# Block 0's normalisation placed inside the end of the mixture, in a two-layer macaron kernel

## The chip, the cores and the metric

One core of one Trainium2 chip runs the whole program. The metric is the device time of one launch in microseconds (us); lower is better. The core has five engines that run their own instruction streams and meet only at semaphores: TensorE (PE in the profile, with its weight loads as PEld), VectorE (DVE), ScalarE (ACT), GpSimd (POOL) and SyncE (SP), which only issues transfers here.

## The reference

The input is 2 sequences of 2048 tokens with 256 features. Every residual branch starts from a layer norm:

```python
x = x + 0.5 * moe(norm(x))      # layer 0, "ffn0a": 32 experts, 4 per token, 160 slots each, and a shared expert
x = x + gla(norm(x))            # layer 0, "attn0": gated linear attention
x = x + 0.5 * moe(norm(x))      # "ffn0b", the weights of ffn0a
x = x + 0.5 * ffn1(norm(x))     # layer 1, "ffn1a": 8 experts, 2 per token
x = x + attn1(norm(x))          # layer 1, a scan over time
x = x + 0.5 * ffn1(norm(x))     # "ffn1b"
```

Of `moe`, this matters: each expert's output rows are scaled and added to their tokens, and the shared expert's output `silu(x @ gate.T) * (x @ up.T) @ down.T` is added for every token.

## The kernel before

Tokens lie on 128 partitions, 32 tiles deep, in `main_x`; 4 tiles are a block, so there are 8 blocks (`NB`). Each stage is a `Block` in which every engine has a list of instructions written by hand; a barrier of all engines stands between two stages. Two such seams matter here: ffn0a to attn0 (whose first half is `project`) and ffn0b to ffn1a. ffn0a and ffn0b are the same code, `moe`.

In `moe` blocks 0, 1, 4, 5, 6, 7 go through the shared expert first (`up`, `gate`, `hidden`, `down`, `keep`; `NF` = 6), then come 32 routed experts, then the shared expert for the two late blocks 2 and 3. Routed outputs can't be added to `main_x`, whose space holds expert weights (`we`) and shared outputs by then, so they are added in HBM, to four tables `ffn_sums`: GpSimd issues 40 scattered adds (`add`, L693), one per piece of 128 rows. Expert e goes to table e % 4; the four tables are complete one after another.

The late part in TensorE's order is: up products of a late block (`up`, L763, into the banks of `ps_a` and `ps_b`), its down products (`down`, L773, into `ps_c` and `ps_d`), and the same again. ScalarE takes the silu (L949), VectorE multiplies (`hidden`, L1069), ScalarE copies the output to `main_x` (`keep_late`, L955). While this runs, SyncE waits for the last pieces of each table and loads block 0 of it (`sp_first`, L1264, two transfers per table) into `main_spare`.

After the barrier, VectorE adds the four tables of block 0 (`dve_first`, L1278, L1281, L1286), takes its statistics (L216, L221); GpSimd turns the variance into 1/deviation (L245 to L248). In attn0 VectorE then writes the normed block (L232), in ffn1a ScalarE does (L2109); TensorE transposes it (L265), ScalarE copies the transpose out of PSUM (L276, L2118), and the first real products follow (L1540 in attn0, L2191 in ffn1a). Blocks 1 to 7 come through `combine.sp` (L1271, eight transfers a block, each half released by VectorE's adds of the block before) and `combine.dve` (L1295, L1304, for late blocks L1300 and L1302). Before block 0's transposes TensorE runs ten passes of products that nobody reads (`warm`, L177), and in attn0 joins two small gate weights (`join_gate_weights`, L1583 and L1587).

Early in ffn0a, SyncE's list is: clear tables (L410), store shared outputs (`shared`, L599), and load the first two groups of expert weights (`load`, L602, 1.5 MB each). `shared_y` has two places: ScalarE's copy for output n waits for the store of output n - 2. SyncE's list has `load(0)` and `load(1)` ahead of `shared(3)`. In ffn0b the loads stand earlier in the list.

## Time and profile before

| | us |
|---|---|
| three timed runs, lowest / median / highest | 1153.76 / 1155.86 / 1157.72 |
| the profiled execution's own time | 1156.85 |
| span of its instructions | 1154.9 |
| TensorE busy | 1023.1 |
| VectorE busy | 723.8 |
| ScalarE busy | 560.0 |
| GpSimd busy | 383.0 |

The profiled execution's own time is 1.95 above its span and 0.99 above the median of the timed runs. Times in the rows count from the start of the span. A row of a timeline is: start, duration, engine, line, operation, what it writes and reads, how many, and in brackets how long its engine had been idle and who released it. PEclk is the granted clock of TensorE as a share of its upper level, so 1.00 is 2.4 GHz and 0.50 is 1.2 GHz.

### The profile page before, as it was taken

The page shows a single profiled execution, that of the slowest core. Times are in us where ns is not written, and L with a number is a line of the kernel's source. Part 1 is how long each engine was busy: PE and PEld are TensorE (multiplying, and loading weights), DVE is VectorE, ACT ScalarE, POOL GpSimd, SP SyncE. Part 2 cuts the span into 40 slices and gives each one's busy share as a digit, 9 for nine tenths or more (in the row PEclk, how much of TensorE's full clock was granted, in tenths as well). Part 3 has the DMA queues.
Part 4 walks back from the last instruction along what each step waited for, and adds up shares of the span by engine and source line. Part 5 has one row for each costly group of instructions (what it writes and reads, how often), then busy time and mean ns, then how long its engine had stood idle before and what let it go on. Part 6 is the DMA issues. An engine that isn't in the chain of part 4 may idle for free. (4 is left out here: it accounts for less than half of the span.)

```text
span 1154.9 us, 17176 instructions
## 1 busy us (share of the span) xinstructions
PE 1023.1 (89%) x5110; PEld 606.1 (52%) x5128; DVE 723.8 (63%) x2529; ACT 560.0 (48%) x1071; POOL 383.0 (33%) x448
## 2 busy tenths in 40 slices
PE   7998899969998799989998989857887799985997
PEld 4755666535565466656666666423333456642343
DVE  4598432147884566754797331168876699964885
ACT  6621333325665745548422333246664655525884
POOL 3006777700000232314017887311101256521110
PEclk9999899999999799999999999968889899997998
DMA  9849987834440802005428887575400000000012
GB/s 326 331 159 306 185 199 182 183 113 146 151 141 13 324 37 91 11 28 173 165 73 157 201 234 132 104 230 181 141 5 1 1 0 1 1 1 0 20 54 73
DMA packets 81127, 140.72 MB, mean 122 GB/s; under 512 B 17776, under 2 KB 48864, under 8 KB 78944
## 3 DMA queue, kind: packets, MB, share of 16 engines
q1 hardware_dynamic: 65696, 117.58, 29.4%
q0 software_dynamic: 15360, 22.29, 13.0%
q8 instruction: 33, 0.54, 0.2%
q14 instruction: 38, 0.31, 0.1%
HBM read 82.17 MB, written 58.72 MB: 122 GB/s over the span
## 5 line engine op out<-in xcount | busy, mean ns | idle before, releaser
L693 POOL DMA_INDIRECT ffn_sums<-ffn0a_xT,ffn0a_into x40 | 62.7, 1567 | 16.0 <-issue 8.8
L693 POOL DMA_INDIRECT ffn_sums<-ffn0b_xT,ffn0b_into x40 | 62.5, 1563 | 14.7 <-issue 9.2
L1721 POOL TENSOR_TENSOR attn_attend_state_m<-attn_attend_state,attn_attend_heads 128x512 f32<-128x512 f32 x15 | 19.1, 1272 | 87.3 <-DVE attn_attend_state L1763 81.8
L2593 PE MATMUL attn_ps_k<-attn_xk,mixing_wk 128*128 128x512 f32 (+1 forms) x96 | 46.7, 610 | 0.0
L2598 PE MATMUL attn_ps_r<-attn_xr,mixing_wr 128*128 128x512 f32 (+1 forms) x96 | 45.2, 593 | 0.7 <-DVE attn_out L2462 0.7
L1143 DVE TENSOR_TENSOR ffn0a_h<-ffn0a_sg,ffn0a_ps_b 128x160 f32<-128x160 f32 x32 | 10.3, 322 | 54.4 <-ACT ffn0a_sg L981 54.3
L2608 PE MATMUL attn_ps_y<-mixing_wv,attn_out 128*128 128x256 f32 (+1 forms) x192 | 43.0, 380 | 1.2 <-DVE attn_out L2462 1.2
L842 PE MATMUL ffn0a_ps_b<-main_x,ffn0a_h 128*32 128x256 f32 (+2 forms) x144 | 43.5, 403 | 0.0
L842 PE MATMUL ffn0b_ps_b<-main_x,ffn0b_h 128*32 128x256 f32 (+2 forms) x144 | 43.5, 403 | 0.0
L820 PE MATMUL ffn0a_ps_b<-ffn0a_early,main_x 128*128 128x160 f32 x256 | 41.3, 305 | 2.1 <-DMA main_x<-w_experts 1.8
L1742 DVE COPY_PREDICATED main_spare<-attn_attend_causal,attn_attend_ps_a 128x1024 f32<-128x1024 int32 x32 | 40.3, 1312 | 4.6 <-issue 3.0
L1143 DVE TENSOR_TENSOR ffn0b_h<-ffn0b_sg,ffn0b_ps_b 128x160 f32<-128x160 f32 x32 | 10.3, 321 | 52.4 <-ACT ffn0b_sg L981 52.3
L2608 PEld LDWEIGHTS attn_ps_y<-mixing_wv,attn_out 128*128 128x128 f32 (+1 forms) x192 | 36.3, 190 | 10.1 <-issue 3.3
L820 PE MATMUL ffn0b_ps_b<-ffn0b_early,main_x 128*128 128x160 f32 x256 | 41.3, 305 | 0.3 <-ACT ffn0b_early L974 0.3
L820 PEld LDWEIGHTS ffn0a_ps_b<-ffn0a_early,main_x 128*128 128x128 f32 x256 | 36.6, 190 | 7.7 <-issue 3.5
L820 PEld LDWEIGHTS ffn0b_ps_b<-ffn0b_early,main_x 128*128 128x128 f32 x256 | 36.6, 190 | 5.7 <-issue 4.2
L2452 DVE TENSOR_TENSOR_SCAN attn_st<-mixing_keep,attn_carry,attn_kr 128x512 f32<-128x512 f32 (+1 forms) x24 | 32.1, 1337 | 9.8 <-ACT attn_kr L2553 9.7
L773 PE MATMUL ffn0a_ps_c<-ffn0a_shared_down,ffn0a_h 128*128 128x256 f32 x112 | 29.0, 405 | 9.8 <-ACT main_x L966 6.9
L1295 DVE TENSOR_TENSOR main_spare<-main_spare 128x1024 f32<-128x1024 f32 x28 | 34.1, 1218 | 4.9 <-DMA main_spare<-ffn_sums 4.9
L1763 DVE SCALAR_TENSOR_TENSOR attn_attend_state<-attn_attend_state,attn_decay,attn_attend_ps_s 128x256 f32<-128x256 f32 x32 | 14.0, 478 | 33.2 <-PE attn_attend_ps_s L1861 33.2
L395 POOL DMA_INDIRECT ffn0a_early<-ffn_rows,ffn0a_token x10 | 12.6, 1256 | 63.5 <-issue 63.2
L1876 PE MATMUL attn_attend_ps_w<-attn_attend_wo,attn_attend_cent 128*128 128x256 f32 x128 | 31.6, 391 | 2.1 <-DVE attn_attend_cent L1757 2.1
(510 smaller groups left out, 2718.9 us busy)
## 6 DMA issues: line engine op xcount, KB each, us to landing
main_spare<-ffn_sums SPq DMA_DIRECT2D x128, 256.0 KB, 3.6
main_x<-w_experts SPq DMA_DIRECT2D x16, 1536.0 KB, 7.1
ffn_sums<-main_lent SPq DMA_DIRECT2D x36, 512.0 KB, 6.3
ffn_sums<-main_x SPq DMA_DIRECT2D x28, 512.0 KB, 4.6
ffn_rows<-ffn0a_early SPq DMA_DIRECT2D x8, 512.0 KB, 9.7
ffn_rows<-ffn0b_early SPq DMA_DIRECT2D x8, 512.0 KB, 2.9
x_out<-main_x SPq DMA_DIRECT2D x8, 512.0 KB, 2.9
main_x<-x_in SPq DMA_DIRECT2D x3, 1024.0 KB, 10.7
```

Source lines behind the costliest of these rows:

```text
L693: g.indirect_dma_start(out=sums[:, :], out_offset=IndirectOffsetOnAxis(ap=into[:, at, j:j + 1], axis=0), in_=ys[:, n % NY, :], in_offset=N ...
L773: ins = mm(ps[:, i, :], h[:, n % 2, m, t * P:(t + 1) * P], wd[:, m, :], start=m == 0, stop=m == 1)
L820: ins = mm(ps_b[:, p, j * CAP:(j + 1) * CAP], we[:, r, n, j, k * F:(k + 1) * F], xgT[:, k, e // ME % 2, e % ME].rearrange("p a b -> p (a b)"),
L842: ins = mm(ps_b[row:row + m, 2 + piece % 2, 0:D], eh[:, p, at:at + m], we[:, r, n, 2, :], start=True, stop=True)
L1143: v.tensor_tensor(eh[:, p, :], esg[:, p, :], ps_b[:, p, CAP:2 * CAP], ALU.mult).then_inc(eh_made, 1)
L1295: v.tensor_tensor(parts[:, half, 0:2], parts[:, half, 0:2], parts[:, half, 2:4], ALU.add)\
L1742: vec.copy_predicated(att[:, p, s].rearrange("p (r n) i -> p r n i", n=2), causal[:].unsqueeze(1).unsqueeze(1).to_broadcast([P, 4, 2, P]), ...
L1876: ins = mm(ps_w[:, s, :], cent[:, 1 - p, k, s, :], wo[:, k, :], start=k == 0, stop=k == KD - 1)
L2452: v.tensor_tensor_scan(st[0:rows, m % 2], keep[0:rows, m:m + 1].to_broadcast([rows, BN]), kr[0:rows, m % 2], carry[0:rows, p, m:m + 1], AL ...
L2593: ins = mm(ps_k[0:rows, m % 2], wk[:, k, at:at + rows], xk[:, p, k, :], start=k == 0, stop=k == KD - 1)
L2598: ins = mm(ps_r[0:rows, m % 2], wr[:, k, at:at + rows], xr[:, p, k, :], start=k == 0, stop=k == KD - 1)
L2608: ins = mm(ps_y[:, t, :], out[0:rows, p, m, t * P:(t + 1) * P], wv[0:rows, m, :], start=m == 0, stop=m == NMH - 1)
```

## The change

Five things are done, the first three at both seams.

1. Block 0's sums and norm move ahead of the barrier. VectorE adds a table between the products of the late blocks (`dve_first(1)`, `(2)`, `(3)`), then takes the statistics and writes the normed block into the last block of `main_x`, whose expert weights are used up by then. GpSimd does its part at the end of `moe`. The norm's buffers and semaphores now live across the stages (`head`). In ffn1a it is now VectorE that writes the normed block, not ScalarE.
2. The late part of TensorE's list is all four `up` first, then all four `down`, and a `down` waits for the copy out of its own bank only (`banks=2`).
3. SyncE issues the table loads of block 1 (`combine.sp(1)`) inside `moe` already. The unread products ahead of attn0 and ffn1a go.
4. In attn0 the transposes of block 0 stand before the second half of the joining of the gate weights, on TensorE and ScalarE alike; the load of the activation table moves into ffn0a, and ffn1a's goes.
5. In ffn0a `load(0)` and `load(1)` stand behind `shared(3)`.

```diff
@@ class Norm
...
+    def xn_of(self, b, p):
+        return self.first_xn if isinstance(b, int) and b == 0 and self.first_xn is not None else self.xn[:, p]
...
-            ins = nc.vector.tensor_scalar(self.xn[:, p, t, :], self.x[:, tile(t), :],
+            ins = nc.vector.tensor_scalar(self.xn_of(b, p)[:, t, :], self.x[:, tile(t), :],
...
@@ def moe, SyncE
+                shared(3)
+                if not ahead:
                     load(0)
                     load(1)
-                for n in range(3, NF):
+                for n in range(4, NF):
                     shared(n)
...
                     combine.sp_first(n)
+                combine.sp(1)
@@ def moe, GpSimd
+                head.pool_start()
+                head.pool(number(0))
@@ def moe, TensorE
-                def down(n, half, ps=ps_y):
+                def down(n, half, ps=ps_y, banks=1):
                     pe.wait_ge(h_made, 2 * n + 2)
-                    after(pe, y_kept, 2 * n + half)
+                    after(pe, y_kept, 2 * n + half + 1 - banks)
...
                 for n in range(NF, NB):
                     for m in range(2):
                         up(n, m, late_ps[m])
+                for n in range(NF, NB):
                     for half in range(2):
-                        down(n, half, late_y[half])
+                        down(n, half, late_y[half], banks=2)
@@ def moe, ScalarE
                         gate(n, m, late_ps[m])
+                if next_table:
+                    s.preload_act_table_set(next_table)
+                for n in range(NF, NB):
                     for half in range(2):
                         keep_late(n, half, late_y[half])
@@ def moe, VectorE
                 dve.wait_ge(piece_made, NP)
-                for n in range(NF, NB):
-                    for m in range(2):
-                        hidden(n, m, (ps_a, ps_b[:, 0:2])[m])
+                late_ps = (ps_a, ps_b[:, 0:2])
+                hidden(NF, 0, late_ps[0])
+                hidden(NF, 1, late_ps[1])
+                combine.dve_first(1)
+                hidden(NF + 1, 0, late_ps[0])
+                combine.dve_first(2)
+                hidden(NF + 1, 1, late_ps[1])
+                combine.dve_first(3)
+                head.dve_moments(number(0), lambda t: t)
+                head.dve_apply(number(0), lambda t: t)
@@ class Combine
-    def dve_first(self):
+    def dve_first(self, n):
         v, parts = self.nc.vector, self.parts
+        if n == 1:
+            v.wait_ge(self.first_landed[0], 32)
+        else:
+            v.wait_ge(self.first_step, n - 1)
+        v.wait_ge(self.first_landed[n], 32)
+        if n < NTAB - 1:
+            v.tensor_tensor(parts[:, :, 0], parts[:, :, 0], parts[:, :, n], ALU.add).then_inc(self.first_step, 1)
+            return
...
@@ def project
-                for b in range(1, NB):
+                for b in range(2, NB):
                     combine.sp(b)
...
-                    combine.dve_first()
-                    ln.dve_moments(j, lambda t: j[0] * BT + t)
-                    ln.dve_apply(j, lambda t: j[0] * BT + t)
                     combine.dve((1, 1, 0), 0)
...
-                s.preload_act_table_set(EXP_AND_LN)
                 act.wait_ge(weights, 8 * 16)
...
-                join_gate_weights()
-                warm(nc, con, ps_t[:, 0, :], 5)
@@ def ffn1
-                if combine:
-                    combine.dve_first()
-                moments(number(0))
+                if not head:
+                    moments(number(0))
...
-                s.preload_act_table_set(SILU)
-                if combine:
-                    ew.cast_constants()
-                act.wait_ge(ln.power_set, 1)
-                apply(number(0), 0)
-                apply(number(0), 1)
+                if not head:
+                    s.preload_act_table_set(SILU)
+                if not head:
+                    apply(number(0), 0)
+                    apply(number(0), 1)
                 turned(number(0))
                 turned16(number(0))
+                if head:
+                    ew.cast_constants()
...
-                warm(nc, con, ps_t[:, 0, :], 5 if combine else 3)
+                if not head:
+                    warm(nc, con, ps_t[:, 0, :], 3)
@@ def macaron_kernel
+        block0_xn = x[:, NT - BT:NT, :]
+        with Scope(nc, "attn0_head") as held:
+            head = Norm(held, nc, x, con, BT, first_xn=block0_xn)
...
+        head = NormWithShift(sc, nc, x, con, BT, first_xn=block0_xn)
...
```

VectorE from the last products of ffn0a to the first of attn0, before (`ffn0a_h` is the hidden layer of the shared expert, `main_spare` the loaded tables):

```order
L1069 TENSOR_TENSOR ffn0a_h<-ffn0a_sg,ffn0a_ps_b 128x512 [waits ffn0a_y_made,ffn0a_gate_made]
L1069 TENSOR_TENSOR ffn0a_h<-ffn0a_sg,ffn0a_ps_a 128x512 [waits ffn0a_y_made,ffn0a_gate_made]
L1069 TENSOR_TENSOR ffn0a_h<-ffn0a_sg,ffn0a_ps_b 128x512 [waits ffn0a_y_made,ffn0a_gate_made]
L577 UNCONDITIONAL_BRANCH
L1418 UNCONDITIONAL_BRANCH [waits barrier_Pool_Activation_PE_DVE_SP_release]
...
L1278 TENSOR_TENSOR main_spare<-main_spare 128x2x512 [waits main_combine0_first_landed1,main_combine0_first_landed0,attn0_project_carry_set]
L1281 TENSOR_TENSOR main_spare<-main_spare 128x2x512 [waits main_combine0_first_landed2,main_combine0_first_step]
L1286 TENSOR_TENSOR main_x<-main_spare 128x512 [waits main_combine0_first_landed3,main_combine0_first_step]
...
L216 BN_STATS attn_project_ln_stats<-main_x 128x6 x4
L221 BN_AGGR attn_project_ln_moments<-attn_project_ln_stats 128x2 x4
L232 TENSOR_SCALAR attn_project_ln_xn<-main_x,attn_project_ln_moments,attn_project_ln_rstd 128x256 [waits attn0_project_ln_rstd_ready]
```

and after:

```order
L1119 TENSOR_TENSOR ffn0a_h<-ffn0a_sg,ffn0a_ps_b 128x512 [waits ffn0a_y_made,ffn0a_gate_made]
L1339 TENSOR_TENSOR main_spare<-main_spare 128x2x512 [waits main_combine0_first_landed1,main_combine0_first_landed0]
L1119 TENSOR_TENSOR ffn0a_h<-ffn0a_sg,ffn0a_ps_a 128x512 [waits ffn0a_y_made,ffn0a_gate_made]
L1339 TENSOR_TENSOR main_spare<-main_spare 128x2x512 [waits main_combine0_first_landed2,main_combine0_first_step]
L1119 TENSOR_TENSOR ffn0a_h<-ffn0a_sg,ffn0a_ps_b 128x512 [waits ffn0a_y_made,ffn0a_gate_made]
L1343 TENSOR_TENSOR main_x<-main_spare 128x512 [waits main_combine0_first_landed3,main_combine0_first_step]
...
L227 BN_STATS attn_head_ln_stats<-main_x 128x6 x4
L232 BN_AGGR attn_head_ln_moments<-attn_head_ln_stats 128x2 x4
L243 TENSOR_SCALAR main_x<-main_x,attn_head_ln_moments,attn_head_ln_rstd 128x256 [waits attn0_head_ln_rstd_ready]
L1474 UNCONDITIONAL_BRANCH [waits barrier_Pool_Activation_PE_DVE_SP_release]
```

The three additions and the norm stand ahead of the barrier now, and two of the multiplications of the late blocks stand behind a wait for a table.

TensorE from the late blocks of ffn0a on, before (`ps_a` and `ps_b` take up products, `ps_c` and `ps_d` down products):

```order
L763 MATMUL ffn0a_ps_a<-ffn0a_xT_late,ffn0a_shared_gate 128x512 [waits ffn0a_h_made,ffn0a_tokens_ready,ffn0a_slots_ready]
L763 MATMUL ffn0a_ps_b<-ffn0a_xT_late,ffn0a_shared_gate 128x512 [waits ffn0a_h_made]
L773 MATMUL ffn0a_ps_c<-ffn0a_shared_down,ffn0a_h 128x256 [waits ffn0a_y_kept,ffn0a_h_made]
L773 MATMUL ffn0a_ps_d<-ffn0a_shared_down,ffn0a_h 128x256 [waits ffn0a_y_kept,ffn0a_h_made]
L763 MATMUL ffn0a_ps_a<-ffn0a_xT_late,ffn0a_shared_gate 128x512 [waits ffn0a_h_made]
L763 MATMUL ffn0a_ps_b<-ffn0a_xT_late,ffn0a_shared_gate 128x512 [waits ffn0a_h_made]
L773 MATMUL ffn0a_ps_c<-ffn0a_shared_down,ffn0a_h 128x256 [waits ffn0a_y_kept,ffn0a_h_made]
L773 MATMUL ffn0a_ps_d<-ffn0a_shared_down,ffn0a_h 128x256 [waits ffn0a_y_kept,ffn0a_h_made]
L1531 UNCONDITIONAL_BRANCH [waits barrier_Pool_Activation_PE_DVE_SP_release]
L1583 MATMUL attn_project_ps_kd<-main_con,main_lent 16x128 [waits main_gate_weights_landed]
L1587 MATMUL attn_project_ps_z<-main_lent,attn_project_lnz 128x128 [waits attn0_project_w1T_kept]
```

and after:

```order
L809 MATMUL ffn0a_ps_a<-ffn0a_xT_late,ffn0a_shared_gate 128x512 [waits ffn0a_h_made,ffn0a_tokens_ready,ffn0a_slots_ready]
L809 MATMUL ffn0a_ps_b<-ffn0a_xT_late,ffn0a_shared_gate 128x512 [waits ffn0a_h_made]
L809 MATMUL ffn0a_ps_a<-ffn0a_xT_late,ffn0a_shared_gate 128x512 [waits ffn0a_h_made]
L809 MATMUL ffn0a_ps_b<-ffn0a_xT_late,ffn0a_shared_gate 128x512 [waits ffn0a_h_made]
L819 MATMUL ffn0a_ps_c<-ffn0a_shared_down,ffn0a_h 128x256 [waits ffn0a_y_kept,ffn0a_h_made]
L819 MATMUL ffn0a_ps_d<-ffn0a_shared_down,ffn0a_h 128x256 [waits ffn0a_y_kept,ffn0a_h_made]
L819 MATMUL ffn0a_ps_c<-ffn0a_shared_down,ffn0a_h 128x256 [waits ffn0a_y_kept,ffn0a_h_made]
L819 MATMUL ffn0a_ps_d<-ffn0a_shared_down,ffn0a_h 128x256 [waits ffn0a_y_kept,ffn0a_h_made]
L1582 UNCONDITIONAL_BRANCH [waits barrier_Pool_Activation_PE_DVE_SP_release]
L1630 MATMUL attn_project_ps_kd<-main_con,main_lent 16x128 [waits main_gate_weights_landed]
L276 MATMUL attn_project_ps_t<-main_con,main_x 128x128 [waits attn0_head_ln_xn_ready]
```

The up products of the second late block stand ahead of the down products of the first, the unread products are gone, and the transposes stand between the two halves of the joining.

SyncE in the front part of ffn0a, before (`main_x<-w_experts` are the weight loads, `ffn_sums<-main_x` the stored shared outputs):

```order
L599 DMA ffn_sums<-main_x 128x1024 [waits ffn0a_y_kept]
L410 DMA ffn_sums<-main_lent 128x1024 x6
L602 DMA main_x<-w_experts 128x3072 [waits ffn0a_x_stored1]
L602 DMA main_x<-w_experts 128x3072
L599 DMA ffn_sums<-main_x 128x1024 [waits ffn0a_y_kept] x3
L602 DMA main_x<-w_experts 128x3072 [waits ffn0a_piece_made] x6
```

and after:

```order
L640 DMA ffn_sums<-main_x 128x1024 [waits ffn0a_y_kept]
L451 DMA ffn_sums<-main_lent 128x1024 x6
L640 DMA ffn_sums<-main_x 128x1024 [waits ffn0a_y_kept,ffn0a_x_stored1]
L643 DMA main_x<-w_experts 128x3072 x2
L640 DMA ffn_sums<-main_x 128x1024 [waits ffn0a_y_kept] x2
L643 DMA main_x<-w_experts 128x3072 [waits ffn0a_piece_made] x6
```

One of the three stores moved ahead of the two loads, and the loads with it behind its wait for ScalarE's copy (`y_kept`).

## Rows read from the trace of the kernel before

**Rows 1.** The page: the span
```profile
span 1154.9 us, 17176 instructions
```

**Rows 2.** Busy time by stretch: us, PE, PEld, DVE, ACT, POOL, PEclk, DMA, GB/s
```profile
257.00:266.00 9.00, 7.65 (x22) 4.80 (x23) 6.64 (x19) 2.44 (x4) 1.33 (x2) 0.62 0.80 271
309.00:322.00 13.00, 13.00 (x48) 7.91 (x47) 10.79 (x23) 8.40 (x17) 1.29 (x2) 1.00 0.46 153
757.00:776.00 19.00, 12.43 (x30) 4.81 (x32) 14.92 (x56) 8.37 (x16) 2.39 (x7) 0.50 0.67 223
776.00:884.00 108.00, 88.48 (x409) 38.84 (x415) 86.17 (x324) 67.02 (x135) 9.06 (x22) 0.87 0.31 97
```

**Rows 3.** TensorE in time, end of ffn0a to attn0: start, us, idle before, releaser
```profile
219.26 1.88 PE L763 MATMUL ffn0a_ps_a<-ffn0a_xT_late,ffn0a_shared_gate 128*128 128x512 f32 x4
...
227.70 1.99 PE L773 MATMUL ffn0a_ps_c<-ffn0a_shared_down,ffn0a_h 128*128 128x256 f32 x8 [1.41 <-DVE ffn0a_h L1069]
...
257.09 1.30 PE L265 MATMUL attn_project_ps_t<-main_con,attn_project_ln_xn 128*128 128x128 f32 x8 [3.82 <-DVE attn_project_ln_xn L232]
259.65 3.75 PE L1540 MATMUL attn_project_ps_z<-attn_project_ln_xT,main_lent 128*128 128x512 f32 x4 [1.26 <-ACT attn_project_ln_xT L276]
```

**Rows 4.** ScalarE in time, same stretch: last copy of ffn0a
```profile
245.49 0.60 ACT L955 ACTIVATE main_x<-ffn0a_ps_d 128x512 f32<-128x512 f32 x1 [2.15 <-PE ffn0a_ps_d L773]
```

**Rows 5.** SyncE queue: first loads of tables 2 and 4, each with its landing times
```profile
L1264 SPq DMA_DIRECT2D main_spare<-ffn_sums x2: 319/376/432, 227.0 to 227.4; - x2
DMA to landing us min/median/max: 3.7/4.8/5.9
...
L1264 SPq DMA_DIRECT2D main_spare<-ffn_sums x2: 319/400/481, 233.1 to 233.5; - x2
DMA to landing us min/median/max: 2.8/2.9/3.1
```

**Rows 6.** VectorE in time, first operations of attn0
```profile
246.53 0.48 DVE L1423 MEMSET attn_project_carry<- 128x512 f32 x1 [5.87 <-PEq L577]
...
248.41 1.22 DVE L1278 TENSOR_TENSOR main_spare<-main_spare 128x1024 f32<-128x1024 f32 x1
...
250.98 1.29 DVE L1286 TENSOR_TENSOR main_x<-main_spare 128x512 f32<-128x512 f32 x2
...
255.65 1.38 DVE L232 TENSOR_SCALAR attn_project_ln_xn<-main_x,attn_project_ln_moments,attn_project_ln_rstd 128x256 f32<-128x256 f32 x4 [1.51 <-POOL attn_project_ln_rstd L248]
257.52 1.22 DVE L1295 TENSOR_TENSOR main_spare<-main_spare 128x1024 f32<-128x1024 f32 x1 [0.49 <-DMA main_spare<-ffn_sums]
...
260.15 1.22 DVE L1295 TENSOR_TENSOR main_spare<-main_spare 128x1024 f32<-128x1024 f32 x1 [0.56 <-DMA main_spare<-ffn_sums]
```

**Rows 7.** Second seam (ffn0b to ffn1a): TensorE, SyncE, VectorE, ScalarE in turn
```profile
720.96 1.88 PE L763 MATMUL ffn0b_ps_a<-ffn0b_xT_late,ffn0b_shared_gate 128*128 128x512 f32 x4
...
760.98 3.58 PE L2191 MATMUL ffn1a_ps_r<-ffn1a_ln_xT,main_router 128*8 128x512 f32 x4 [1.11 <-ACT ffn1a_ln_xT L2118]
...
L1264 SPq DMA_DIRECT2D main_spare<-ffn_sums x2: 320/376/432, 737.2 to 737.6; - x2
DMA to landing us min/median/max: 3.2/3.5/3.8
...
757.00 1.22 DVE L1295 TENSOR_TENSOR main_spare<-main_spare 128x1024 f32<-128x1024 f32 x1 [3.11 <-DMA main_spare<-ffn_sums]
...
766.02 2.06 ACT L2109 ACTIVATE ffn1a_ln_xn<-main_x,ffn1a_shift,ffn1a_ln_rstd 128x256 f32<-128x256 f32 x4
```

**Rows 8.** The wait in ffn0a: TensorE, then VectorE
```profile
116.29 3.75 PE L773 MATMUL ffn0a_ps_c<-ffn0a_shared_down,ffn0a_h 128*128 128x256 f32 x8 [6.17 <-ACT main_x L966]
...
119.48 0.24 DVE L1147 TENSOR_TENSOR ffn0a_own<-ffn0a_early,main_con 128x80 f32<-128x80 f32 x1 [5.40 <-DMA ffn0a_early<-ffn_rows,ffn0a_token]
```

**Rows 9.** GpSimd in time, a scattered add of ffn0a that waited, and the last
```profile
147.18 1.55 POOL L693 DMA_INDIRECT ffn_sums<-ffn0a_xT,ffn0a_into  x1 [2.01 <-DMA ffn_sums<-ffn0a_xT,ffn0a_into]
...
226.79 1.57 POOL L693 DMA_INDIRECT ffn_sums<-ffn0a_xT,ffn0a_into  x1 [0.30 <-issue]
```

More of the change, by code:

```diff
@@ L130, in staged, with each @@
     peeled(range(n - 2, n + 2))
-def each(eng, body, n):
-    body((0, 0, 0))
-    body((1, 1, 0))
+def each(eng, body, n, start=0):
+    for b in range(start, 2):
+        body(number(b))
     with eng.Fori(0, n // 2 - 1) as i:
@@ L433, in sp_x, with moe @@
         sp.dma_start(tables(self.sums)[0][:, rows], x[:, rows]).then_inc(self.x_stored, 16)
-def moe(nc, name, x, con, w, table, sums, gathered, added, turn_no, spare, combine, arriving=None,
-        load_next=None, zero=None, ahead=None):
+def moe(nc, name, x, con, w, table, sums, gathered, added, turn_no, spare, combine, head, arriving=None,
+        load_next=None, zero=None, ahead=None, next_table=None):
     with Scope(nc, name) as sc:
@@ L1414, in _ @@
             def _(pool):
-                ln.pool_start()
-                each(pool, ln.pool, NB)
+                each(pool, ln.pool, NB, 1)
             @block.vector
@@ L1884, in _, with attn0 @@
                 steps(pe, step)
-def attn0(nc, name, x, con, w, gw, ew, combine, spare, ahead):
+def attn0(nc, name, x, con, w, gw, ew, combine, spare, ahead, head):
     with Scope(nc, name) as sc:
@@ L1957, in _ @@
                 if combine:
-                    for b in range(1, NB):
+                    for b in range(2, NB):
                         combine.sp(b)
@@ L2270, in work @@
                         up(j0, 0)
-                warm(nc, con, ps_t[:, 0, :], 5 if combine else 3)
+                if not head:
+                    warm(nc, con, ps_t[:, 0, :], 3)
                 ln.pe(number(0))
@@ L2669, in macaron_kernel @@
             mw = MixWeights(nc, held, w)
-            ffn1(nc, "ffn1a", x, con, ew, combine[1], load_next=mw.load)
+            ffn1(nc, "ffn1a", x, con, ew, combine[1], load_next=mw.load, head=head)
             attn1(nc, "attn1", x, con, mw)
```

113 lines of the change are left out of this document (60 added, 53 removed).

## The prediction

> **What bounds the kernel now.** I read the span first [rows 1]: the profiled execution takes 1156.85 us, of which 1154.9 are span. Then the busy times by stretch [rows 2]: in the middle of attn0's first half TensorE is busy for 13.00 of 13.00 us, so that half is one row of TensorE work, and whatever lets it begin earlier ends it earlier. In ffn1a TensorE is busy for 88.48 of 108 us and VectorE for 86.17: a pipeline of short steps that pass work from engine to engine, none of them full, which also moves as a whole with its start. So the two seams are read as starts. The timeline of TensorE over the first seam [rows 3] shows what the reader is to see: the late part begins at 219.26, waits 1.41 for VectorE before the first down products (two shorter waits for ScalarE's copy are like it), and the first real product of attn0 begins at 259.65. Between the last copy of ffn0a, which ends at 245.49 + 0.60 = 246.09 [rows 4], and that product lie 13.6 us in which only short steps run one after another: barrier, table additions, statistics, 1/deviation, norm, transposes, copy.
>
> **Parts 1 to 4, first seam.** The question is what ends ffn0a once the norm is in front of the barrier.
> TensorE alone: one late block's up products take 227.70 - 1.41 - 219.26 = 7.0 [rows 3], two take 13.9, so they end near 233.1; four down groups at some 1.9 (1.99 for the first) end near 240.8, and ScalarE's last copy (0.6) at 241.5.
> VectorE: its list is strict, and the multiplication for the second late block now stands behind the wait for tables 1 and 2. The second load of table 2 starts at 227.4 and the longest landing of the pair is 5.9 [rows 5], so 233.3. Then, with 1.22 for an addition [rows 6] and 0.69 for a multiplication (half of the 1.29 of two operations of that size, a little more): addition to 234.6, multiplication to 235.3, third table to 236.5, second multiplication to 237.3. The last two down groups wait for that one: they run to 241.1, the copy to 241.9. Table 4 lands at 233.5 + 3.1 = 236.6, so VectorE is free for the last additions at 237.35. From the start of the last additions to the end of the norm it takes 255.65 + 1.38 - 250.98 = 6.05 today, GpSimd's 1.5 included [rows 6], and these are the same operations. The norm ends at 243.4. VectorE ends ffn0a, 2.7 before 246.09.
> Behind the barrier: today the first step of VectorE starts 0.44 after 246.09 [rows 4, 6], so attn0 would start its engines near 243.7. TensorE has two transposes of a gate weight (some 0.4), block 0's eight (1.30), then the copy out of PSUM with the waits on both sides (1.26) [rows 3], and the copy of the joined weights now stands behind it on ScalarE, 0.3: first product at 247.0. It was at 259.65, so 12.7.
> Block 1 must come along. Its table loads are issued when the first half of block 0 is added, at 238.0. Today VectorE takes them 257.52 - 250.98 = 6.5 after the last additions began, and the second half 2.63 later [rows 6]: 243.9 and 246.5. VectorE has its five preparations first, 248.41 - 246.53 = 1.9, and is ready at 245.7, behind the landing; the second half at 247.7, against 260.15. That is 12.4. I take 12.5 for the seam. It needs no engine to be faster: 10.0 is block 0's chain that now runs beside late products, 2.7 is the shorter late part. The joining, the activation table load and the statistics hide below TensorE's products; if that cover were gone they would cost the 1.3 to 1.9 that VectorE's preparations take.
>
> **The same at the second seam.** The late part starts at 720.96 [rows 7]. Here GpSimd is later against TensorE: the last load of table 4 starts at 737.6 and lands by 3.8 later, 741.4. The last additions start at 741.45, the norm ends 6.05 later, 747.5. The late part of today is the same code and has its copy end 246.09 - 219.26 = 26.8 after its start, at 747.8. So almost nothing comes from the barrier, 0.3. Behind it: the barrier 0.3, transposes 1.3 to 2.0, copy 1.1: the scores' product at 750.5, against 760.98, 10.5. Block 1: first half taken 6.3 to 6.5 after the last additions, 747.9 (today 757.00), second half some 2.8 later, 750.6; additions 2.0, statistics 1.8 and GpSimd's chain 1.6, so ScalarE writes block 1 at 756.0 against 766.02. That is 10.0, and I take it, as both chains meet there. The constants that ScalarE casts (0.9) now lie below the scores' product.
>
> **Part 5.** TensorE waits 6.17 in ffn0a for ScalarE's copy, which waits for a store behind the 3 MB of weights [rows 8]. The wait goes. What is late next is VectorE's wait for the first gathered rows, until 119.48, 3.2 after TensorE resumed: TensorE would start the experts about 1 us earlier. But ffn0a's end is VectorE's chain above, hung on table 4, and that on GpSimd's last add, which starts at 226.79 with the usual 0.30 of issue before it [rows 9]. From the first gather on GpSimd only ever waits for landings, as at 147.18 (2.01), never long for TensorE. So the value is 0. Bounds: a gain of 6.2, the whole wait, if gathers and adds are issued faster beside the moved loads; a loss of 2.0, one more landing wait, if the loads collide with gathers that they do not meet today. I take 0, by the last add's row.
>
> **The clock.** The granted clock is at its lower level for most of 257 to 266 and for all of 757 to 776 (0.50) [rows 2], after idle stretches of TensorE of 3.82 [rows 3] and about 5, although unread products ran just before. So these did not keep the clock up, and taking them out costs nothing by these rows. After the change TensorE idles 2.7 between its last down product and the gate weights, with light work behind: I can't tell whether the clock falls. If it stays up, 257 to 266 shrinks by up to 0.38 x 9 = 3.4, of which VectorE, nearly full there, lets perhaps 2 through. I count 0. The Trainium skill ("TensorE: Matmul & The Clock Gate", What's actually happening) says that the throttled state is the default and activity releases it; by that rule removing the unread products speaks against this change; by it alone the stage that starts sparse stays slow, which is rival C below, and by the rows the sum stands.
>
> **Sum.** 1156.85 - 12.5 - 10.0 - 0 = 1134.3 for a profiled execution. The profiled one lies 1.0 above the median of the timed runs, so 1133.4.
>
> **Rivals.**
> A, more: the clock stays up at the first seam (2 to 3) or GpSimd ends earlier in ffn0a (part 5, up to 6.2; TensorE's own end, 1.9 before VectorE's in the first seam, lets 2 to 4 through, more only if it is earlier too). For it: the shorter idle stretch. Against: nothing in GpSimd's list moves. 1133.4 - 4 = 1129.4.
> B, less: block 1 is the next thing late. Its loads are released earlier, but land no faster; if they cost 4 more at each seam than the 6.5 taken here, or VectorE's waits for tables delay the late products, the chain of later blocks keeps only 8 and 6. For it: VectorE already waits 3.11 for block 1's loads at the second seam [rows 7]. Against: its preparations cover the landing at the first. 1156.85 - 14 - 1.0 = 1141.9.
> C, slower: ffn1a begins with sparse work and no unread products, and its clock stays at the lower level as in 757 to 776 for its whole length. Its 88.48 busy at a mean of 0.87 would be 88.48 x 0.87 / 0.50 = 154 against 108: a loss of 46, so 1179. It turns the sign once 0.50 lasts for over half of those 108 us. Against: the clock rose at 776 today without help.
> D, the change doesn't do what it says: a table's landing delays the norm until it is later than the barrier was, by 10 or more, and only the removed waits remain: some 1152.
>
> **Chances.** Forecast 0.62, A 0.17, B 0.15, C 0.03, D 0.03. The range reaches from A to B: 1127 to 1142. A measurement of this kernel tells 0.3%, 3.5 us, from no change. Faster by more than that: all but C and part of D, 0.96; same 0.01; slower 0.03.
>
> **What the profile after would show.** Last additions near 237.4 and the norm's end near 243.4 on VectorE; TensorE's first product of attn0 near 247; four up groups without a gap, then down groups with one gap of about 1 for VectorE; in ffn0b the norm near 747.5 less the first seam's 12.5; ffn1a's first scores 22 to 23 earlier than 760.98; no 6 us gap near 110 and the last scattered add still near 226.8. The prediction is wrong if block 1 in either stage waits for loads longer than today, if GpSimd's last add moves, or if the clock in ffn1a differs from 0.87.

## Result and the profile after

The changed kernel takes 1141.27 us (median of 4 runs, 1135.99 to 1146.33), against 1156.79 us for the kernel before (4 runs, 1153.76 to 1158.03) on the same chip. The ratio is 0.9863, with a 95% interval of 0.9826 to 0.9899: 15.5 us faster. I measured it once more, unaltered, beside the last three experiments: 1146.59 us (5 runs), ratio 0.9914 (0.9881 to 0.9948), 10.0 us faster. The forecast was 1133.4, a gain of 22.5, in a range of 1127 to 1142. So the direction is right, the range holds the first measurement and not the second, and of the forecast gain 7.0 us are missing in the first and 12.5 in the second, a third and more than a half. The profiled execution took 1146.33 us, with a span of 1143.0.

TensorE over the first seam of the changed kernel, in time, as in [rows 3] (start, duration, instruction, and in brackets the idle time ahead of it and what ended it):

```profile
219.86 1.88 PE L809 MATMUL ffn0a_ps_a<-ffn0a_xT_late,ffn0a_shared_gate 128*128 128x512 f32 x4
...
231.88 1.88 PE L809 MATMUL ffn0a_ps_b<-ffn0a_xT_late,ffn0a_shared_up 128*128 128x512 f32 x4
233.60 1.89 PE L819 MATMUL ffn0a_ps_c<-ffn0a_shared_down,ffn0a_h 128*128 128x256 f32 x8
...
237.39 1.99 PE L819 MATMUL ffn0a_ps_c<-ffn0a_shared_down,ffn0a_h 128*128 128x256 f32 x8 [0.18 <-DVE ffn0a_h L1119]
239.22 1.89 PE L819 MATMUL ffn0a_ps_d<-ffn0a_shared_down,ffn0a_h 128*128 128x256 f32 x8
249.29 0.59 PE L1630 MATMUL attn_project_ps_kd<-main_con,main_lent 128*16 128x128 f32 x2 [8.18 <-PEq L618]
249.67 1.91 PE L276 MATMUL attn_project_ps_t<-main_con,main_x 128*128 128x128 f32 x8
...
253.21 3.78 PE L1591 MATMUL attn_project_ps_z<-attn_project_ln_xT,main_lent 128*128 128x512 f32 x4 [0.47 <-ACT main_lent L1576]
```

The late part is as forecast: 13.7 us of up products without a gap, then the down products with one gap of 0.18. Then TensorE is idle for 8.18 us. VectorE, ScalarE and GpSimd of the same stretch:

```profile
238.16 1.29 DVE L1343 TENSOR_TENSOR main_x<-main_spare 128x512 f32<-128x512 f32 x2 [0.83 <-DMA main_spare<-ffn_sums]
...
242.83 1.38 DVE L243 TENSOR_SCALAR main_x<-main_x,attn_head_ln_moments,attn_head_ln_rstd 128x256 f32<-128x256 f32 x4 [1.51 <-POOL attn_head_ln_rstd L259]
249.43 0.48 DVE L1479 MEMSET attn_project_carry<- 128x512 f32 x1 [5.23 <-PEq L618]
...
251.32 1.22 DVE L1352 TENSOR_TENSOR main_spare<-main_spare 128x1024 f32<-128x1024 f32 x1
...
253.30 1.22 DVE L1352 TENSOR_TENSOR main_spare<-main_spare 128x1024 f32<-128x1024 f32 x1
...
241.15 0.60 ACT L1002 ACTIVATE main_x<-ffn0a_ps_d 128x512 f32<-128x512 f32 x1 [1.13 <-PE ffn0a_ps_d L819]
...
241.75 1.05 POOL L259 TENSOR_TENSOR attn_head_ln_rstd<-attn_head_ln_ve,attn_head_ln_power 128x4 f32<-128x4 f32 x1
```

The last additions start at 238.16 (forecast 237.4), the norm is done at 242.83 + 1.38 = 244.21 (forecast 243.4), ScalarE's last copy at 241.75. Nothing that the stage computes is left after 244.21, and yet attn0 starts at 249.29: 5.1 us in which no engine works. Before the change that step took 0.44 for VectorE [rows 4, 6]. The second seam shows the same:

```profile
738.44 0.20 POOL L316 TENSOR_TENSOR main_ln_shift<-main_ln_neg_mean,main_ln_rstd 128x4 f32<-128x4 f32 x1
...
738.39 1.38 DVE L243 TENSOR_SCALAR main_x<-main_x,main_ln_moments,main_ln_rstd 128x256 f32<-128x256 f32 x4 [1.54 <-POOL main_ln_rstd L314]
745.13 1.22 DVE L1352 TENSOR_TENSOR main_spare<-main_spare 128x1024 f32<-128x1024 f32 x1 [5.35 <-PEq L618]
...
745.13 1.94 PE L276 MATMUL ffn1a_ps_t<-main_con,main_x 128*128 128x128 f32 x8 [5.79 <-PEq L618]
...
748.18 3.58 PE L2224 MATMUL ffn1a_ps_r<-ffn1a_ln_xT,main_router 128*8 128x512 f32 x4 [1.11 <-ACT ffn1a_ln_xT L2150]
```

The norm is done at 739.77, ScalarE's last copy (not shown) at 739.98, and TensorE and VectorE start at 745.13, 5.15 after the copy. The busy times by stretch (us, then PE, PEld, DVE, ACT, POOL, granted clock, DMA share, GB/s), beside [rows 2]:

```profile
244.00:246.00 2.00, 0.00 (x0) 0.00 (x0) 0.21 (x1) 0.00 (x0) 0.00 (x0) 0.69 1.03 361
247.00:249.20 2.20, 0.00 (x0) 0.00 (x0) 0.00 (x0) 0.00 (x0) 0.00 (x0) 0.50 0.00 0
249.30:253.20 3.90, 3.44 (x14) 2.74 (x14) 3.68 (x7) 1.78 (x3) 0.00 (x0) 0.50 0.00 0
764.00:872.00 108.00, 89.47 (x415) 38.79 (x412) 86.69 (x325) 66.47 (x134) 8.34 (x20) 0.87 0.29 94
```

In the idle stretch the 16 DMA engines are full until 246 with block 1's table loads, which the change issues in front of the stage's end, and empty from 247 on. The granted clock has fallen to 0.50, 1.2 GHz, before attn0 begins. The loads were my first explanation of the 5.1 us.

### The profile page after: what moved, and what is told of

The parts are those of the page before. It is cut to its first block and busy times, and to the rows that moved or that the text cites. A ratio compares the mean times of both kernels' runs of the same rounds, so it can differ in the third digit from the quotient of the medians.

```text
span 1143.0 us, 17155 instructions
## 1 busy us (share of the span) xinstructions
PE 1020.0 (89%) x5108; PEld 607.1 (53%) x5108; DVE 724.4 (63%) x2533; ACT 556.5 (49%) x1066; POOL 378.3 (33%) x448
```

## Experiments

For every version below I also give the two seams of its profiled execution: from TensorE's first late up product (219.26 in the kernel before [rows 3]) to TensorE's first step of the next stage, and from there to the first product that uses the normed block 0 (259.65). These lengths leave out how long the mixture took up to its late part, which differs by up to 6 us between executions (the first seam's late part starts between 213.8 and 219.9 in the 14 profiles).

| version | median, us | before, same chip | ratio (95%) | first seam | second seam |
|---|---|---|---|---|---|
| before | 1156.79 | | | 27.13 + 13.26 | 27.13 + 12.89 |
| changed | 1141.27 | 1156.79 | 0.9863 (0.9826 to 0.9899) | 29.43 + 3.92 | 26.59 + 3.05 |
| changed, again | 1146.59 | 1156.57 | 0.9914 (0.9881 to 0.9948) | 29.11 + 3.91 | 32.67 + 3.05 |
| e1, loads behind the end | 1152.55 | 1154.28 | 0.9977 (0.9959 to 0.9994) | 29.07 + 3.91 | 33.28 + 3.05 |
| e2, no GpSimd drain | 1131.40 | 1154.28 | 0.9797 (0.9778 to 0.9817) | 24.77 + 2.98 | 23.68 + 2.38 |
| e3, half of the loads behind | 1145.85 | 1154.28 | 0.9937 (0.9918 to 0.9956) | 28.69 + 3.92 | 29.22 + 3.06 |
| e4, one load, late | 1151.18 | 1154.28 | 0.9965 (0.9943 to 0.9987) | 29.22 + 3.91 | 31.83 + 3.05 |
| e5, before, no GpSimd drain | 1155.81 | 1156.89 | 0.9989 (0.9968 to 1.0009) | 27.19 + 13.05 | 27.18 + 12.92 |
| e6, before, late GpSimd step | 1168.04 | 1156.89 | 1.0090 (1.0068 to 1.0111) | 33.46 + 13.05 | 33.45 + 12.02 |
| e7, e2 with weights first | 1135.17 | 1156.89 | 0.9795 (0.9751 to 0.9840) | 24.82 + 3.24 | 23.79 + 2.64 |
| e8, before, ups first alone | 1144.90 | 1156.89 | 0.9875 (0.9839 to 0.9912) | 21.74 + 13.05 | 21.75 + 12.89 |
| e9, changed, ups late | 1151.26 | 1156.57 | 0.9959 (0.9940 to 0.9978) | 32.44 + 3.91 | 32.87 + 3.06 |
| e10, e9, no GpSimd drain | 1137.20 | 1156.57 | 0.9829 (0.9789 to 0.9870) | 27.74 + 2.64 | 27.79 + 2.17 |
| e11, norm's step on ScalarE | 1138.07 | 1156.57 | 0.9851 (0.9807 to 0.9895) | 23.82 + 3.09 | 29.59 + 3.05 |

**The first theory: the loads in flight.** A stage ends with a drain instruction on each engine and a barrier of semaphores, which the language writes at the end of a block. Theory D said that a drain waits for loads in flight. e1 takes the loads away from the end:

```diff
@@ def moe, SyncE
-                combine.sp(1)
@@ def project and def ffn1, SyncE
-                for b in range(2, NB):
+                for b in range(1, NB):
                     combine.sp(b)
```

> The changed kernel, but block 1's eight table loads are issued in the next stage again, as the first thing that SyncE does there. Nothing else differs. In the changed kernel both next stages start 5.1 us after the norm's end (249.3 after 244.2, and 745.1 after 740.0), and both times these loads are in flight. Theory D (the stage's end waits for the loads in flight): both gaps shrink to 0.3 to 0.5, so attn0's engines start near 244.6 and ffn1a's some 10 us earlier than 745.1 in all; the loads go out at 244.7 and land from 247.5 to 250, so VectorE's first half of block 1 in attn0 moves only from 251.3 to about 249.7, and the product of attn0 with the normed block from 253.2 to about 248.6. The time falls by 3 to 8 us against the changed kernel's 1141.3: 1133 to 1138. Theory F (the switch is long for another reason, as the code of the longer stage or the semaphores that are cleared): the gaps stay 5, block 1 comes 4 later, the time is 1143 to 1148.

VectorE in e1, from the norm to block 1's first half:

```profile
239.24 1.38 DVE L243 TENSOR_SCALAR main_x<-main_x,attn_head_ln_moments,attn_head_ln_rstd 128x256 f32<-128x256 f32 x4 [1.51 <-POOL attn_head_ln_rstd L259]
245.84 0.48 DVE L1478 MEMSET attn_project_carry<- 128x512 f32 x1 [5.22 <-PEq L618]
...
251.26 1.23 DVE L1351 TENSOR_TENSOR main_spare<-main_spare 128x1024 f32<-128x1024 f32 x1 [3.45 <-DMA main_spare<-ffn_sums]
...
254.41 1.23 DVE L1351 TENSOR_TENSOR main_spare<-main_spare 128x1024 f32<-128x1024 f32 x1 [1.08 <-DMA main_spare<-ffn_sums]
```

No load is in flight and the gap is still 5.22. Theory D is refuted, and so is the thought that the switch queues for the DMA engines. What e1 shows instead is what the loads in front are worth: VectorE now waits 3.45 for them (and 1.08 for the second half), so block 1's second half starts 254.41 - 216.63 = 37.8 after the late part's start, against 253.30 - 219.86 = 33.4 in the changed kernel. e1 is 1.7 us faster than before, where the changed kernel is 10.0 to 15.5. Theory F had the gap and the 4 us of block 1 right, but its time, 1143 to 1148, is missed too: no forecast had the loads worth that much.

e3 and e4 give the same answer in doses:

> The changed kernel with four of block 1's eight loads (its first half, 1 MB) in front of the stage's end, the other four behind it. Theory D (the end waits for loads in flight): the packets of four loads last until about 243 to 244 in the first seam instead of 246.9, so attn0's engines start near 245.5 to 246.5 instead of 249.3, 2.4 us after the last packet as in the changed kernel; ffn1a 2 to 3 us earlier against its own norm. Time 1135 to 1139. Theory F (another reason): the gap stays 5.1, no gain.

> The changed kernel with one single load of block 1 (256 KB) in front of the stage's end, held back until the norm is done (244.2), so that it is the last thing before the end and alone on the DMA engines; the other seven go out in the next stage. Theory D (the end waits for the loads in flight to complete): the gap from the norm's end to attn0's first step is at least the landing of that one load, 2.7 or more, so 247.0 to 248. Theory Q (the switch itself needs the DMA engines, for code for instance, and queues behind 2 MB of packets): one load keeps the 16 engines busy for less than 1 us, so the gap is 0.4 to 1.3, attn0 starts at 244.6 to 245.5. Theory F (another reason): 5.1 as now.

The gap on VectorE is 5.23 in e3 (245.88 is its first step of attn0) and 5.22 in e4 (243.13), whatever is in flight. D and Q expected a length that varies with the loads; it is a constant. The times follow the number of loads issued in front of the end instead: 1.7 us faster than before with none, 3.1 with one, 8.4 with four, 10.0 and 15.5 with eight.

**The second theory: GpSimd's drain.** The language can leave out the drain instruction of GpSimd alone:

```diff
-        with nc.Block() as block:
+        with nc.Block(no_gpsimd_drain=True) as block:
```

> The changed kernel with the mixture's end written without GpSimd's drain instruction (every other engine keeps its own). Block 1's loads stay in front of the end. Theory D1 (GpSimd's drain is what waits for the loads in flight): both gaps fall from 5.1 to about 0.4 while the loads land as now, so 4 to 5 us fall away at each end and the time is 1131 to 1135. Theory D2 (SyncE's own drain waits for the loads that SyncE issued) and theory F (another reason): the gaps stay at 5.1 and the time at 1141.

VectorE, then TensorE, in e2:

```profile
240.46 1.38 DVE L243 TENSOR_SCALAR main_x<-main_x,attn_head_ln_moments,attn_head_ln_rstd 128x256 f32<-128x256 f32 x4 [1.51 <-POOL attn_head_ln_rstd L259]
242.37 0.48 DVE L1479 MEMSET attn_project_carry<- 128x512 f32 x1 [0.54 <-PEq L618]
...
242.24 0.38 PE L1630 MATMUL attn_project_ps_kd<-main_con,main_lent 128*16 128x128 f32 x2 [3.41 <-PEq L618]
...
245.22 3.78 PE L1591 MATMUL attn_project_ps_z<-attn_project_ln_xT,main_lent 128*128 128x512 f32 x4 [0.47 <-ACT main_lent L1576]
```

The gap is 0.54 on VectorE, at the second seam 0.41, and the time is 1131.40, as expected of D1. But with e1 the reason that D1 gives, the loads, is excluded. What was left was the constant itself, and the engine it counts from. In the changed kernel GpSimd's last step ends at 241.75 + 1.05 = 242.80 and TensorE starts at 249.29, 6.5 later; at the second seam 738.64 and 745.13, 6.5. Theory P: GpSimd's drain takes some 6 us from GpSimd's own last step on. In the kernel before it lay below the late products. A row of the kernel before that I had not used says so, the first step of GpSimd in attn0:

```profile
246.74 0.10 POOL L238 MEMSET attn_project_ln_eps<- 128x4 f32 x1 [18.39 <-POOLq L577]
```

GpSimd had been idle for 18.39 us at that stage end. The 0.44 that I took from [rows 4, 6] was the price of an end at which GpSimd had been done for long, and the change gives GpSimd a step 1.4 us before the end. Two experiments on the kernel before test P from both sides: e5 leaves out the drain where P says that it is hidden, and e6 adds one late GpSimd step where it is not.

> The kernel before with the mixture's end written without GpSimd's drain instruction, nothing else. In the kernel before, GpSimd's last step in a mixture ends some 18 us before the stage ends (GpSimd idle 18.4 and 15.8 us there). Theory P (GpSimd's drain takes some 6 us from GpSimd's own last step on, and is hidden while GpSimd ends early): no change, 1153 to 1156, gaps at the two ends as before, 0.3 to 0.5. Rival R (the drain costs in any case, by other means than the gap): 5 or more us faster.

> The kernel before with one more GpSimd instruction, a memset of 128x4 (0.1 us), as GpSimd's last step in three stages: in both mixtures behind ScalarE's last copy, and in attn0's first half behind ScalarE's last copy there. This measures the price of the late step by itself, with no table load in flight at any of the three ends. Theory P: each mixture's end grows from some 0.4 to some 6.5 us counted from the memset, so each costs about 6 more. In attn0's first half GpSimd issues no DMA; if the drain's length hangs on the DMA that GpSimd has issued in its stage (P1), that end stays under 2 us; if it is a fixed price (P2), it is 6.5 there too. The time: 1154 + 12 = 1166 by P1, 1154 + 18 = 1172 by P2. Theory D (only loads in flight count): no change, 1154.

```diff
@@ def moe, GpSimd, behind its last scattered add
+                pool.wait_ge(y_kept, 2 * NB)
+                nc.gpsimd.memset(touched[:], 0.0)
@@ def project, GpSimd
+                pool.wait_ge(kd_kept, NB)
+                nc.gpsimd.memset(touched[:], 0.0)
```

GpSimd and TensorE in e6, at the end of ffn0a and at the end of attn0's first half:

```profile
244.60 0.10 POOL L721 MEMSET ffn0a_touched<- 128x4 f32 x1 [17.60 <-ACT main_x L958]
...
251.18 0.59 PE L1589 MATMUL attn_project_ps_kd<-main_con,main_lent 128*16 128x128 f32 x2 [7.28 <-PEq L578]
...
376.22 0.10 POOL L1422 MEMSET attn_project_touched<- 128x4 f32 x1 [22.06 <-ACT attn_kd L1520]
...
376.66 3.56 PE L177 MATMUL attn_attend_ps_w<-main_con 128*128 128x512 f32 x4 [1.13 <-PEq L1411]
```

e5 is 0.9989, no change. In e6 TensorE starts 6.48 us after the end of a memset of 0.10 us (251.18 - 244.70), both mixtures' seams grow by 6.3, and the kernel by 11.2. At the end of attn0's first half the same memset costs nothing: TensorE starts 0.34 after it. So the long drain belongs to the mixtures, as P1 expected, and not to every stage. GpSimd issues scattered adds and gathers by DMA in the mixtures and none in attn0's first half. That this is the cause is argued, not shown: the stages differ in other things too.

e11 then keeps the drain, the loads and everything else, and moves only the step. In ffn0a ScalarE computes 1/deviation behind its last copy; ffn0b is left as it is:

```diff
@@ def moe, GpSimd
                 head.pool_start()
-                head.pool(number(0))
+                if next_table != EXP_AND_LN:
+                    head.pool(number(0))
@@ def moe, ScalarE, behind keep_late
+                if next_table == EXP_AND_LN:
+                    act.wait_ge(head.power_set, 1)
+                    head.act_rstd(number(0))
```

> The changed kernel with 1/deviation of block 0 computed by ScalarE (a logarithm and an exponential, behind its last copy) instead of GpSimd, in ffn0a alone; ffn0b keeps GpSimd's step. The stage's end and its drain stay as they are, and block 1's loads are in flight as before. Theory P (the drain counts from GpSimd's own last step): in ffn0a that is now near 228, so the drain is hidden, and attn0 starts 0.4 after the norm's end, near 244.4 instead of 249.3, while ffn1a still starts 6.5 after GpSimd's step: 1136.5 in all. Theory E (any stage end with GpSimd's DMA work behind it and loads in flight takes 5 once the last engine has arrived): attn0 near 249, 1141.

ScalarE, VectorE and TensorE at the first seam of e11, then GpSimd and TensorE at its second:

```profile
239.79 0.21 ACT L268 ACTIVATE attn_head_ln_rstd<-attn_head_ln_lnv 128x4 f32<-128x4 f32 x1
...
240.04 1.38 DVE L243 TENSOR_SCALAR main_x<-main_x,attn_head_ln_moments,attn_head_ln_rstd 128x256 f32<-128x256 f32 x4 [0.92 <-ACT attn_head_ln_rstd L268]
...
241.74 0.38 PE L1634 MATMUL attn_project_ps_kd<-main_con,main_lent 128*16 128x128 f32 x2 [2.80 <-PEq L618]
...
730.50 0.20 POOL L316 TENSOR_TENSOR main_ln_shift<-main_ln_neg_mean,main_ln_rstd 128x4 f32<-128x4 f32 x1
...
737.19 1.94 PE L276 MATMUL ffn1a_ps_t<-main_con,main_x 128*128 128x128 f32 x8 [8.68 <-PEq L618]
```

One execution holds both cases. Where ScalarE does the step, TensorE starts 0.3 after the norm's end (241.42); where GpSimd does it, 6.5 after GpSimd's last step. The seam is 33.02 - 26.91 = 6.1 shorter than in the changed kernel's second profile. The time is 1138.07, 8.5 below the changed kernel on the same chip, where 4.8 was expected; by the ratios it is 0.9851 against 0.9914, with intervals that overlap, and against the first measurement of the changed kernel, 0.9863, it is next to nothing. So it is the trace that decides here and not the time: P holds, E is refuted.

**What each part is worth.** e7 undoes part 5 on top of e2:

> The version without GpSimd's drain (1131.4) with part 5 undone: the first two expert weight loads of ffn0a are issued ahead of the fourth shared output's store again. What part 5 is worth by itself. My prediction's term is 0 (bounds: a gain by part 5 of 6.2, a loss of 2.0): 1131 expected, 1129 to 1138 possible; TensorE's wait of some 6 us near 116 comes back, and the wait for the first gathered rows (4.4 us near 116 to 120 in the changed kernel) goes.

The ratios are 0.9795 and 0.9797 (the medians, on two chips, 1135.17 and 1131.40): no worth of part 5 can be seen, but by the two intervals a worth of up to some 6 us either way is not excluded. The trace of e7 has the wait for ScalarE's copy back (7.01, until 114.31) and no wait for the gathered rows, where e2 waits 5.49 for them, until 118.15. In the changed kernel the wait of 6.17 [rows 8] is down to 0.78, and TensorE instead waits 4.36 for the first gathered rows, which the prediction named as next:

```profile
110.92 1.97 PE L819 MATMUL ffn0a_ps_c<-ffn0a_shared_down,ffn0a_h 128*128 128x256 f32 x8 [0.78 <-ACT main_x L1013]
...
120.03 2.96 PE L839 MATMUL ffn0a_ps_a<-main_con,ffn0a_early 128*128 128x128 f32 x12 [4.36 <-DMA ffn0a_early<-ffn_rows,ffn0a_token]
```

> The kernel before with the late up products ahead of the late down products on TensorE and ScalarE, in both mixtures, and nothing else of the change. The late part then has no wait for VectorE: 13.9 for the ups and 7.7 for the downs, the last copy 22.2 after the start against 26.8. At the first seam that is 4.6 earlier, and block 0's additions behind the end move with it (their tables land at 236.6, before 241.5). At the second, table 4 lands at 741.4 and the end comes at 743.2, also 4.6 earlier. Expected 1154.3 - 9.2 = 1145; if the shorter late part is given back later, up to 1150.

On TensorE (ScalarE's copies move behind its gates in the same way):

```diff
                 for n in range(NF, NB):
                     for m in range(2):
                         up(n, m, late_ps[m])
+                for n in range(NF, NB):
                     for half in range(2):
-                        down(n, half, late_y[half])
+                        down(n, half, late_y[half], banks=2)
```

TensorE at the first seam of e8, the last up products to attn0's first step:

```profile
231.53 1.88 PE L763 MATMUL ffn0a_ps_b<-ffn0a_xT_late,ffn0a_shared_up 128*128 128x512 f32 x4
233.24 1.89 PE L773 MATMUL ffn0a_ps_c<-ffn0a_shared_down,ffn0a_h 128*128 128x256 f32 x8
...
238.42 1.89 PE L773 MATMUL ffn0a_ps_d<-ffn0a_shared_down,ffn0a_h 128*128 128x256 f32 x8
241.25 0.38 PE L1585 MATMUL attn_project_ps_kd<-main_con,main_lent 128*16 128x128 f32 x2 [0.94 <-PEq L577]
```

The order alone shortens each seam by 5.4 (27.13 to 21.74, and to 21.75) and the kernel by 12.0, where 4.6 and 9.2 were expected. No measurement here tells it apart from the whole change (0.9875 against 0.9863 and 0.9914). e9 and e10 take the order out again:

> The changed kernel with the order of the late products undone on TensorE and ScalarE (the second late block's up products behind the first one's down products again), the rest of the change kept, GpSimd's drain too. The additions and the norm then stand behind the second late block's later gates: last additions near 240.0, GpSimd's step ends near 244.6, and 6.5 of drain make attn0 start near 251.1, 1.8 later than 249.3; the same at the second seam. Expected 1141.3 + 3.6 = 1145. If instead the late order is worth its own 5.4 per seam, as alone on the kernel before, it is 1152.

> The same with the mixture's end written without GpSimd's drain. Without the drain the end is where TensorE's and ScalarE's late part ends, as in the kernel before, near 246.1, with the norm near 246.0: attn0 starts near 246.5 against 242.3 in the version without drain and with the ups first (1131.4). Expected 1131.4 + 2 x 4.2 = 1140; so without the drain the order is worth 8, with it some 4.

e9 is 5.3 us faster than before and e10 19.4. So with the drain exposed the norm in front of the end (with block 1's loads and all the rest of the change) brings 5.3 alone and -2 to +3.5 on top of the order; without it, 19.4 alone and 10.9 on top of the order. The order is worth 4.7 with the drain (e9 against the changed kernel on its chip; against the first measurement, by the ratios, it would be 11) and 5.8 without it, or 3.7 by the ratios. Expected were 3.6 and 8, so e9 came out as the sum with the drain had it, within that scatter, and e10 lower. Parts 3 and 4 were not tried alone: no run puts back only the unread products or the old order of transposes and joining. e9's first seam is 1.2 longer than the 31.2 expected: GpSimd's step ends 25.9 after the late part's start, and TensorE starts 6.5 after that.

> The changed kernel once more, unaltered, beside the next three on one chip. Its first measurement was 1141.3, a ratio of 0.9863 to the kernel before; again 0.984 to 0.989. Both stage ends should again last 6.46 us from GpSimd's last step to TensorE's first.

The unaltered kernel came out at 0.9914, outside the 0.984 to 0.989 expected, though the two intervals overlap. Both ends again last 6.5 us from GpSimd's last step (6.50 and 6.49). The first seam repeats to 0.3 us; the second is 6.1 longer. There VectorE waits for the tables again (8.62 for the second, 0.68 for the fourth), TensorE waits 3.27 for VectorE, and GpSimd's step stands behind it: GpSimd's last scattered add starts 10.7 us after the late part began, where it was 4.6 in the first profile and 10.2 in the kernel before. VectorE and TensorE there:

```profile
732.54 1.22 DVE L1339 TENSOR_TENSOR main_spare<-main_spare 128x1024 f32<-128x1024 f32 x1 [8.62 <-DMA main_spare<-ffn_sums]
...
736.15 3.42 PE L819 MATMUL ffn0b_ps_c<-ffn0b_shared_down,ffn0b_h 128*128 128x256 f32 x8 [3.27 <-DVE ffn0b_h L1119]
```

## Why the prediction was right or wrong

**TensorE's and VectorE's part in front of the end: right.** From the late part's start, the forecast had the last additions at 18.1 and the norm's end at 24.1; it was 18.3 and 24.35.

**The stage's end: wrong, and this is the step that failed.** The text says "Behind the barrier: today the first step of VectorE starts 0.44 after 246.09", and takes the same for the end after the change. It was 5.1. The row was read for the two engines that wait behind the end and not for all five that arrive at it. The step's DMAs and what they pass were counted, and GpSimd's own place at the end was not. The price is shown by e2: 1131.40, a gain of 22.9 us against 22.5 forecast. Its first seam is 27.75, where the forecast had 247.0 - 219.26 = 27.7. That the total agrees to 0.4 us is luck in part: e2's second seam is 14.0 shorter than in the kernel before, where 10.0 was forecast, and of the 26.6 us that its two seams give in the profiles only 22.9 arrive in the medians. It is luck, too, that the changed kernel's first measurement lies in the range: the price of the drain was in no rival, and the upper end of the range is the time of rival B, whose reason is another one (below).

**Behind the end: right in kind, 0.6 too low.** The forecast had 3.3 us from attn0's start to the first product, the changed kernel 3.92, e2 2.98. In the changed kernel the granted clock is 0.50 in the whole stretch, 1.2 GHz, after 8.18 us without a product; the eight transposes take 1.91 us, against 1.30 in the kernel before [rows 3]. In e2 TensorE was idle for 3.41 only and they take 1.15. I had counted 0 for the clock: right for the idle stretch of 2.7 that I forecast (e11 idles for 2.80 and needs 3.09 to the first product), 0.9 short for the one that came (3.92 against 2.98). Over the first 9 us of attn0 the granted clock is 0.62 in e2, as in 257 to 266 of the kernel before [rows 2], and 0.50 in the changed kernel. So nothing here shows a loss by the unread products that went.

**The second seam: the number right once, by luck, the reasons not.** Forecast 10.0 shorter, measured 10.4 in the first profile and 4.3 in the second. The forecast counted 26.8 to the next stage's start, with table 4's landing last. The first profile has 26.59 because GpSimd was 5.5 earlier against TensorE, and the drain then took back 4.8; the second, where GpSimd was as late as in the kernel before, has 32.67, 5.9 more than forecast: the drain and 1 us.

**Block 1 and the late products (rival B): a part of it came, and cost little.** In attn0 VectorE takes block 1's halves at 251.32 and 253.30 without a wait, 2.0 apart, as forecast; in ffn1a it takes the first at 745.13 without a wait. Issuing the loads in front of the end is needed: e1 puts them behind it and keeps 1.7 of the 10.0 to 15.5 us. The other half of B, VectorE's waits for tables that delay the late products, did come at the second seam of the second profile: TensorE waits 3.27 there. It did not set the end: ScalarE's last copy ends at 741.93, the norm at 742.85, and ffn1a starts at 748.20, behind the drain. So B's time, 1141.9, is close to the first measurement for another reason than B's.

**Part 5: nothing against it.** The term was 0. e7 shows none, to within some 6 us, about as wide as the gain of 6.2 that the forecast allowed. The last scattered add of ffn0a, by which the term was taken as 0, starts at 227.58 in the changed kernel and at 226.79 before [rows 9]: 7.7 and 7.5 behind the late part's start.

**Rivals A, C and D.** ffn1a keeps its clock, 0.87 in 764 to 872 with TensorE busy for 89.47 of 108 us, as in [rows 2]; C did not come. D did not come, nor did A.

**The rest of the sum.** The seams of the first profile are 7.04 + 10.38 = 17.4 shorter, the span is 11.9. The difference is 0.6 in front of the first seam, 4.0 between the seams and 0.9 behind the second. The 4.0 lie in ffn0b, where TensorE waits 2.17 and 0.94 for expert weights. Over the same stretch (first product behind the first seam to the second late part) the other versions lie between 1.9 less and 3.5 more than the kernel before, so the 4.0 is at the edge of the scatter, and I leave it open whether a part of it is the change's.

## What to carry to other kernels

The end of a stage here came when its latest engine had arrived, and GpSimd arrived only with its drain: before moving a small step in front of a barrier, look at how long each of the five engines has been idle there, and ask what the engine that gets the step has to do before it counts as arrived. Here a step of 1.5 us on GpSimd exposed some 5 us at each of two ends, and the same step on ScalarE (tried at the first) or the end without GpSimd's drain (at both) gave them back. Try the parts of a change alone: reordering the late products, a few lines, brought as much as the whole change did with its exposed drain. The best version is e2, 1131.40 us, 0.9797 of the kernel before.

## What the runs showed of the hardware

GpSimd's drain at the end of a mixture takes 6.5 us from GpSimd's last step to the next stage's first, in every profile in which it is exposed: 6.5 in the changed kernel at both seams, 6.5 in e11 at the second, 6.48 in e6. It is the same whatever loads are in flight (6.5 in e1, e3 and e4 too) and whatever the step's own length (1.05 us or 0.10). At the end of attn0's first half it is at most 0.34. At the end of attn1, in the kernel before, it is at most 4.9: GpSimd's last step ends there at 1040.36, VectorE's at 1044.92, and TensorE starts at 1045.24 (GpSimd, VectorE, TensorE):

```profile
1040.16 0.20 POOL L2421 TENSOR_TENSOR attn_y_shift<-attn_y_mean,attn_rstd 128x4 f32<-128x4 f32 x1
...
1043.69 1.23 DVE L2488 TENSOR_TENSOR main_x<-main_x,attn_yg 128x1024 f32<-128x1024 f32 x1
...
1045.24 5.03 PE L177 MATMUL ffn1b_ps_t<-main_con 128*128 128x512 f32 x6 [8.49 <-PEq L2383]
```

No row of the kernel before gives the price itself. The Trainium skill ("Runtime: NRT & Kernel Launch", Instruction fetch mechanics) has a rule that could also have explained an idle stage switch: a taken branch to code outside the window that is held forces a fetch by DMA. The trace speaks against it here: the changed kernel's profile has no instruction packet between 240 and 250, though it has them elsewhere, and the branches are the same in e2, where the gap is 0.5.

The other thing is the scatter. The kernel's mixtures reach their late part up to 6 us apart from one execution to the next, with nearly the same instructions up to there, and GpSimd's last scattered add in ffn0b stands 4.6 to 12.2 us behind TensorE at the start of the late part. A term that hangs on one such distance, as my second seam did on table 4, is no better than that.
